# Leaving out seventeen unread products at the end of a decoder layer

## The chip, the cores and the metric

The kernel runs on one core of a Trainium2 chip. The metric is the time of one execution on the device in microseconds (us), as the median of several executions. TensorE is the matrix engine, VectorE and ScalarE work element by element, GpSimd does small element work, and SyncE's queue issues the transfers.

## The reference, cut to what matters

Eight sequences of 128 tokens with 512 features pass through one decoder layer with a layer norm behind each of three parts:

```python
x = _layernorm(x + _L0_attn_ref(x, qkvw, qkvb, ow, ob))      # 32 heads of 16 features
x = _layernorm(x + _L0_xattn_ref(x, ctx, ctx, 0, mask))      # 32 heads on 8 key and value heads
x = _layernorm(x + _L0_ffn_ref(x, weight, bias, gate_w, in_cs, out_cs))
```

The third part is a layer with ternary weights and a router over 8 experts:

```python
routing = softmax(xf @ gate_w.T)            # 8 numbers for each token
out = (xf * (routing @ in_cs)) @ sign(weight).T * (routing @ out_cs) + bias
```

## The kernel before, in words

The eight sequences go in four groups of two (i = 0 to 3). Work is split into two threads of steps. Thread A is the projections and the self attention of a group; thread B is the cross attention and the routed layer of a group. Thread C prepares weights once. `ORDER` (lines 55 to 113) is one list written by hand, in which the steps of all threads are interleaved; each engine walks through the whole list in that order and issues its own share of every step. So the order on each engine is fixed, and engines meet only at semaphores.

A step is named by thread, group, name and indices. In the last group of thread B, which is the end of the kernel, these names matter (b is the sequence in its group, u a half of the heads):

- `st`: the cross scores (line 1275), and their exponential on ScalarE (line 758)
- `pv b,u`: values by probabilities (line 1284), copied to `wide_b` by ScalarE (line 771)
- `ot b,u`: transposes of that back (`quarter`, line 1102); VectorE divides by the sums and adds the residual, and with u = 1 takes the variance (lines 994 to 1004)
- `n2 b`: the second layer norm, in halves (line 861); GpSimd takes the root (lines 605 and 609)
- `cx b,h`: transposes of x2 (line 1102), copied by ScalarE (line 794)
- `rl`, `rt`, `rr`: the router's logits (line 1297), their sum over four parts (line 1304), and the transpose of the exponentials (line 1308), with copies and an exponential on ScalarE (lines 798, 802, 805) and the maximum on VectorE (line 1011)
- `is b,h`: the routing by the input scales, contracted over 8 rows (line 1315); VectorE multiplies x2 by it (line 1024)
- `os b`: the routing by the output scales, again over 8 rows (line 1319)
- `ff b,h`: half of the output features of the ternary layer, from the high part (line 1327) and the low part (line 1331) of the input; VectorE scales, adds and takes the variance (lines 1040 to 1046)
- `n3 b`: the last layer norm and the store of the output (lines 566 and 568)

Beside the real products TensorE does unread ones. `UNREAD` (lines 116 to 129) gives for a step how many are put ahead of it, and `unread` (line 1105) issues them:

```python
held = swT if step[1] == NG - 1 and step[2] not in ("xt", "q") else wH
for _ in range(UNREAD.get(step, 0)):
    pe.matmul(dst, held[:, 0, 0:P], held[:, 0, 0:H], start=True, stop=True)
```

Each is a product of 128 x 128 by 128 x 512, written to a bank of PSUM that nobody reads before it is written again; in the profile they stand at line 1109. Behind the place `LEFT` in the list (the end of thread A) they all go to one bank that the self attention has left (lines 1122 to 1124), after a wait for that bank's last reader, which is long past in the stretch in question. The place of an unread product in TensorE's order is ahead of the real products of its step and ahead of that step's own waits.

Of the kernel before, what the change touches and what calls it, by code (L numbers as in the profile page):

```python
# [18 lines left out]
B = 8  # L19
# [26 lines left out]
def steps(table):  # L46

    out = []
    for token in table.split():
# [80 lines left out]

# [1268 lines left out]
```

## Time and profile before

| | us |
|---|---|
| median of 3 executions | 357.45 |
| lowest, highest | 356.92, 360.22 |
| the profiled execution | 357.36 |
| its span, first to last instruction | 354.9 |
| TensorE busy in the span | 330.6 |
| VectorE, ScalarE, GpSimd busy | 250.1, 191.6, 132.1 |
| mean granted clock of TensorE | 0.966 |

The profile describes one execution. Busy time of TensorE counts products whose ends are modelled and which overlap, so a busy engine is not one at its peak. The granted clock is 1.00 at the full level of 2.4 GHz and 0.50 at 1.2 GHz. The chain of work that ended last is followed back from the last instruction, at each step to what released it.

### The profile page before, as it was taken

The page shows a single profiled execution, that of the slowest core. Times are in us where ns is not written, and L with a number is a line of the kernel's source. Part 1 is how long each engine was busy: PE and PEld are TensorE (multiplying, and loading weights), DVE is VectorE, ACT ScalarE, POOL GpSimd, SP SyncE. Part 2 cuts the span into 40 slices and gives each one's busy share as a digit, 9 for nine tenths or more (in the row PEclk, how much of TensorE's full clock was granted, in tenths as well). Part 3 has the DMA queues.
Part 4 walks back from the last instruction along what each step waited for, and adds up shares of the span by engine and source line. Part 5 has one row for each costly group of instructions (what it writes and reads, how often), then busy time and mean ns, then how long its engine had stood idle before and what let it go on. Part 6 is the DMA issues. An engine that isn't in the chain of part 4 may idle for free. (4 is left out here: it accounts for less than half of the span.)

```text
span 354.9 us, 7999 instructions
## 1 busy us (share of the span) xinstructions
PE 330.6 (93%) x2835; PEld 242.5 (68%) x2835; DVE 250.1 (70%) x839; ACT 191.6 (54%) x387; POOL 132.1 (37%) x214
## 2 busy tenths in 40 slices
PE   6789989999999999999999999999989999998993
PEld 6789866688756784876576958775655676643572
DVE  2842585248998735699998347899964868898636
ACT  4923835541358758342756874316789627456420
POOL 4382462325611432343554224432226635212301
PEclk9699999999999999999999999999999999899956
DMA  7945880376951016856620165763501063200001
GB/s 269 369 162 175 246 217 5 100 208 179 235 161 36 14 35 173 229 170 144 166 86 17 28 171 163 210 155 85 134 7 37 2 166 111 85 6 0 3 0 59
DMA packets 26360, 42.77 MB, mean 121 GB/s; under 512 B 7469, under 2 KB 18361, under 8 KB 24017
## 3 DMA queue, kind: packets, MB, share of 16 engines
q1 hardware_dynamic: 26009, 41.72, 42.0%
q8 instruction: 22, 0.36, 0.4%
q10 hardware_dynamic: 312, 0.55, 0.4%
q14 instruction: 17, 0.14, 0.1%
HBM read 29.48 MB, written 12.32 MB: 118 GB/s over the span
## 5 line engine op out<-in xcount | busy, mean ns | idle before, releaser
L752 ACT ACTIVATE pa<-bank_a 128x512 f32<-128x512 f32 x64 | 35.9, 601 | 15.0 <-PE bank_a L1206 13.4
L981 DVE CUSTOM_DVE_ANT_0 x<-bank_b,mraw 128x128 bf16<-128x128 f32 x192 | 42.2, 284 | 1.0 <-PE bank_b L1264 0.8
L890 DVE TENSOR_REDUCE nma<-bank_a 128x4 f32<-128x512 f32 x64 | 40.5, 681 | 1.6 <-PE bank_a L1189 1.2
L1095 PE MATMUL bank_a<-xH,wH 128*128 128x256 f32 x128 | 36.9, 289 | 0.6 <-DVE xL L871 0.6
L1096 PE MATMUL bank_a<-xL,wH 128*128 128x256 f32 x128 | 36.0, 281 | 0.0
L1097 PE MATMUL bank_a<-xH,wL 128*128 128x256 f32 x128 | 35.9, 281 | 0.0
L758 ACT ACTIVATE pb<-bank_b 128x512 f32<-128x512 f32 x54 | 30.0, 603 | 6.6 <-PE bank_b L1275 3.7
L881 DVE SCALAR_TENSOR_TENSOR qr<-bank_a,bqk,qkp 128x256 f32<-128x256 f32 x32 | 14.0, 478 | 24.7 <-ACT qkp L723 24.7
L628 POOL TENSOR_TENSOR qkp<-qr,qkp 128x512 bf16<-128x512 f32 x16 | 18.6, 1166 | 32.1 <-DVE qkp L886 32.1
L723 ACT ACTIVATE qkp<-bank_a,bqk 128x256 bf16<-128x256 f32 x32 | 13.4, 471 | 29.9 <-PE bank_a L1097 27.1
L743 ACT ACTIVATE bank_b<-mT 128x512 f32<-128x512 f32 x48 | 27.8, 608 | 2.4 <-DVE x2T L1051 1.1
L1095 PEld LDWEIGHTS bank_a<-xH,wH 128*128 128x128 f32 x128 | 24.3, 190 | 1.0 <-DVE xL L871 0.9
L1096 PEld LDWEIGHTS bank_a<-xL,wH 128*128 128x128 f32 x128 | 24.4, 190 | 0.2
L1097 PEld LDWEIGHTS bank_a<-xH,wL 128*128 128x128 f32 x128 | 24.2, 189 | 0.0
L1220 PE MATMUL bank_a<-pa,va 128*32 128x128 f32 x512 | 23.2, 281 | 0.4 <-ACT wide_a L765 0.2
L1189 PE MATMUL bank_a<-ks,qs 96*128 96x128 bf16 x256 | 21.4, 220 | 2.0 <-DVE nma L890 1.5
L1189 PEld LDWEIGHTS bank_a<-ks,qs 96*128 96x128 bf16 x256 | 15.8, 98 | 10.5 <-issue 5.3
L605 POOL TENSOR_SCALAR rsb<-mvb 128x1 f32<-128x1 f32 x16 | 3.6, 222 | 51.9 <-DVE mvb L852 35.9
L1109 PE MATMUL bank_a<-swT 128*128 128x512 f32 x67 | 22.8, 442 | 0.0
L1206 PE MATMUL bank_a<-qs,ks 99*128 99x128 bf16 x256 | 22.1, 220 | 0.5 <-DVE x L906 0.4
L1206 PEld LDWEIGHTS bank_a<-qs,ks 99*128 99x128 bf16 x256 | 15.3, 98 | 8.9 <-issue 6.5
L1275 PE MATMUL bank_b<-qx,kx 99*128 99x512 bf16 x54 | 18.4, 384 | 1.3 <-ACT bank_b L743 0.9
(216 smaller groups left out, 825.3 us busy)
## 6 DMA issues: line engine op xcount, KB each, us to landing
scr_q<-qkp SPq DMA_DIRECT2D x8, 384.0 KB, 3.3
qs<-scr_q SPq DMA_DIRECT2D x8, 384.0 KB, 4.4
scr_k<-qkp SPq DMA_DIRECT2D x8, 384.0 KB, 2.9
ks<-scr_k SPq DMA_DIRECT2D x8, 384.0 KB, 4.7
scr_x<-xp SPq DMA_DIRECT2D x8, 384.0 KB, 2.7
qx<-scr_x SPq DMA_DIRECT2D x8, 384.0 KB, 4.0
wraw<-in_L_attn_attn_qkvw_dram SPq DMA_DIRECT2D x2, 1024.0 KB, 8.9
qs<-scr_q SPq DMA_DIRECT2D x8, 256.0 KB, 4.8
```

Source lines behind the costliest of these rows:

```text
L743: act.activation(pb_bank(i, *of)[:].rearrange("p (r t) -> p r t", r=4), held, ACT.Copy).then_inc(*rb.is_laid(i, *of))
L752: act.activation(pa[:, n % NP, :], pa_bank(i, *step)[:], ACT.Exp, scale=HD ** -0.5).then_inc(*ra.is_empty(i, *step))
L758: act.activation(pb[:, n % NPB, :], pb_bank(i, *step)[:], ACT.Exp).then_inc(*rb.is_empty(i, *step))
L890: dve.tensor_reduce(nma[:, b, 4 * j:4 * j + 4], pa_bank(i, *step)[:].rearrange("p (m t) -> p m t", m=KT), AX.X, ALU.max, negate=True).then ...
L981: last = dve.tensor_tensor_reduce(unread[:, part * P:(part + 1) * P], pb_bank(i, *step)[:, r * P:(r + 1) * P], mraw[:], -1.0, -LOWEST, ALU ...
L1095: pe.matmul(dst, lh, rh, start=kt == 0, stop=False)
L1096: pe.matmul(dst, lh, rl_, start=False, stop=False)
L1097: last = pe.matmul(dst, ll, rh, start=False, stop=kt == KT - 1)
L1109: pe.matmul(dst, held[:, 0, 0:P], held[:, 0, 0:H], start=True, stop=True)
L1189: last = pe.matmul(dst[:, m * P:(m + 1) * P], qs[0:SR, b, j, m, :], ks[0:SR, b, j, m, :], start=True, stop=True)
L1206: last = pe.matmul(dst[:, m * P:(m + 1) * P], ks[0:SM, b, j, m, :], qs[0:SM, b, j, m, :], start=True, stop=True)
L1220: last = pe.matmul(dst[m * VW:(m + 1) * VW, (j % 4) * P:(j % 4 + 1) * P], values(va, b, j * KT + m), pa[:, n % NP, m * P:(m + 1) * P], sta ...
```

## The change

In the table `UNREAD` the last nine entries are left out. They stand for seventeen unread products: two ahead of `pv` 1,1, one ahead of `ot` 1,1, two, four and two ahead of `rl`, `rt` and `rr` of sequence 0, three ahead of `cx` 1,0, one ahead of `rt` of sequence 1 and two ahead of `is` 1,0. The list of steps and everything else stay.

```diff
-          ('B', 3, 'ot', 0, 0): 4, ('B', 3, 'ot', 0, 1): 4, ('B', 3, 'st', 1, 5): 3, ('B', 3, 'pv', 1, 1): 2,
-          ('B', 3, 'ot', 1, 1): 1, ('B', 3, 'rl', 0): 2, ('B', 3, 'rt', 0): 4, ('B', 3, 'rr', 0): 2,
-          ('B', 3, 'cx', 1, 0): 3, ('B', 3, 'rt', 1): 1, ('B', 3, 'is', 1, 0): 2}
+          ('B', 3, 'ot', 0, 0): 4, ('B', 3, 'ot', 0, 1): 4, ('B', 3, 'st', 1, 5): 3}
```

## Rows read from the trace of the kernel before

**Rows 1.** The page: busy us, share, instructions of each engine; clock in 40 slices

```profile
PE 330.6 (93%) x2835; PEld 242.5 (68%) x2835; DVE 250.1 (70%) x839; ACT 191.6 (54%) x387; POOL 132.1 (37%) x214
...
PEclk9699999999999999999999999999999999899956
```

**Rows 2.** Busy time by stretch: start, end, length, engines (instructions), clock, DMA

```profile
296.80:300.00 3.20, 3.20 (x27) 2.22 (x27) 3.17 (x7) 2.27 (x5) 1.05 (x2) 1.00 0.48 139
300.20:303.40 3.20, 3.20 (x10) 2.10 (x9) 0.80 (x3) 2.59 (x6) 0.30 (x1) 0.50 0.92 260
...
330.80:334.30 3.50, 3.32 (x16) 2.11 (x16) 2.36 (x8) 1.02 (x5) 0.78 (x2) 1.00 0.00 0
334.30:337.60 3.30, 3.30 (x25) 2.08 (x24) 1.75 (x5) 2.19 (x6) 1.27 (x1) 1.00 0.01 2
337.70:341.00 3.30, 3.30 (x15) 2.58 (x14) 1.57 (x6) 0.63 (x3) 0.00 (x0) 0.50 0.00 0
```

**Rows 3.** TensorE's instructions in order of time, before the first fall

```profile
298.47 1.12 PE L1319 MATMUL bank_b<-ocf,rT 8*128 8x512 f32 x2
```

**Rows 4.** The chain that ended last, in order of time: start, us, what

```profile
332.19 0.07 DVE nl L1011
...
333.75 0.40 PE bank_a L1102 x2
...
334.47 1.08 PE bank_b L1315 x8
335.55 0.36 PE bank_b L1297 x8
335.91 1.05 PE bank_a L1319 x2
336.96 0.43 PE bank_a L1109
337.39 0.12 PE bank_b L1304 x2
337.51 0.79 PE bank_a L1327 x4
338.30 0.85 PE bank_a L1331 x4
...
340.22 1.15 PE bank_a L1315 x4
341.37 0.85 PE bank_b L1315 x4
342.22 1.71 PE bank_b L1319 x2
...
345.08 0.87 PE bank_b L1331 x4
```

**Rows 5.** Groups of instructions, 330.8 to 334.3: count, busy us, mean ns, idle

```profile
L1109 PE MATMUL bank_a<-swT 128*128 128x512 f32 x9 | 2.8, 424 | 0.0
```

**Rows 6.** TensorE's instructions in order of time, in the tail

```profile
326.34 0.71 PE L1109 MATMUL bank_a<-swT 128*128 128x512 f32 x2
327.47 1.07 PE L1284 MATMUL bank_b<-pb,vx 128*32 128x512 f32 x8 [0.42 <-ACT pb L758]
...
348.13 0.63 PE L1331 MATMUL bank_a<-swT,zL 128*128 128x256 f32 x4
```

**Rows 7.** Instructions of all engines in order of time, in the tail

```profile
328.59 0.60 ACT L771 ACTIVATE wide_b<-bank_b 128x512 f32<-128x512 f32 x1 [1.27 <-PE bank_b L1284]
...
329.34 0.63 PE L1102 MATMUL bank_a<-idf,wide_b 128*128 128x128 f32 x4
...
333.18 0.73 DVE L861 TENSOR_SCALAR x<-x,mvb,rsb 128x256 f32<-128x256 f32 x2 [0.15 <-POOL rsb L609]
...
339.40 0.27 ACT L805 ACTIVATE rT<-bank_b 8x128 f32<-8x128 f32 x1 [1.30 <-PE bank_b L1308]
```

## The prediction

> **What bounds the kernel now.** I read the page first, then the granted clock by stretches, then TensorE's own instructions in order of time over the last 30 us, and last the chain of work that ended last over the same stretch. The change touches nothing before 326 us of a span of 354.9 us, so only the last 29 us can move, apart from chance.
>
> The page's clock line shows full level nearly everywhere, with a weak spot in slice 35 and lower digits in slices 39 and 40 [rows 1]. The stretches sharpen that: the level is 0.50 from 300.2 to 303.4, is 1.00 again before the tail, stays 1.00 through 334.3 to 337.6, and is 0.50 from 337.7 [rows 2]. What TensorE did before each fall is alike: in 296.8 to 300.0 and in 334.3 to 337.6 it is marked busy throughout, but much of it is the routing products with 8 rows (lines 1315 and 1319) [rows 3, 4]. Between 330.8 and 334.3, still at full level, nine of the 16 products recorded are unread ones, 2.8 us of busy time in 3.5 us [rows 2, 5]. The reader should see there that the real work alone would be a handful of short products.
>
> The chain says which engine the end waits for. Up to about 333.7 it runs through ScalarE and VectorE (softmax copies, the second normalisation). From 333.75 to 345.95 it is TensorE almost without a break: transposes, routing products, output scales, the ternary layer's first halves [rows 4]. That is where a level of the clock is worth time.
>
> **The change part by part.** Seventeen products of 512 columns go, and with them seventeen weight loads, which lie beside products. No wait is added, no other engine's queue changes, no transfer moves.
>
> The direct gain, product by product:
> - Two before `pv` of group 1: they run at 326.34 and the real product starts at 327.47 when the exponential is ready [rows 6]. Gain 0.
> - One before `ot` 1,1: the transposes wait for ScalarE's copy that starts at 328.59 and takes 0.60, so until 329.19; they start at 329.34, so 0.15 after it [rows 7]. Gain 0, at most 0.15.
> - Two, four and two before `rl`, `rt`, `rr` of sequence 0: the logits' maximum waits its turn on VectorE behind the variance of sequence 1 and runs at 332.19 on the chain, whatever TensorE does before it [rows 4]. Gain 0.
> - Three before `cx` 1,0: they end at 333.75, and VectorE's first half of x2 ends near 333.55 (two instructions of 0.73 together from 333.18), a start latency ahead of the transposes [rows 4, 7]. Gain 0, at most 0.2.
> - One before `rt` of sequence 1: on the chain, 0.43 from 336.96. Part of that is latency that the next product would have in its place; nine unread ones take 2.8, so one is 0.31 [rows 4, 5]. Gain 0.33, between the two and nearer to the many.
> - Two before `is` 1,0: 0.85 on the chain at the lower level, but the real product then waits for ScalarE's copy of the routing weights, 339.40 + 0.27 = 339.67; with the 0.15 to start that the transposes took above, 339.82. It stands on the chain from 340.22 and its record starts at most 0.07 earlier, near 340.15 [rows 4, 7]. Gain 0.33.
>
> Sum of the direct gain: 0.66.
>
> **The price is the clock.** Without the nine products between 330.8 and 334.3 TensorE has left there the two products of `rt`, one of `rr` and the first transposes of `cx` 1,0: less than it had in either stretch before a fall [rows 2, 3, 5]. I therefore expect the level to fall between the end of the router's products (330.8) and the routing products (334.4), and to stay at 0.50 as it does from 337.7, since the work behind it is the same. How early inside that bracket matters little, as TensorE is off the chain there. The chain then pays the lower price from 334.4 to 337.7, and the same kernel shows both prices:
> - `is` of sequence 0, two steps: 1.08 at the full level; its twin for sequence 1 is 1.15 + 0.85 = 2.00 at half [rows 4]. +0.92.
> - `rl` of sequence 1: 0.36, no row at half level; between +0 and +0.36 (doubled). The routing rows come near doubling, so +0.36.
> - `os` of sequence 0: 1.05 against 1.71 [rows 4]. +0.66.
> - `rt` of sequence 1: 0.12, doubled at most. +0.12.
> - `ff` 0,0: 0.79 + 0.85 = 1.64, already mostly at half level; two such groups at 0.87 are 1.74 [rows 4]. +0.10.
> - The four transposes of `cx` 1: 0.40 for two, so 0.80 doubled adds between 0 (the fall comes behind them) and 0.80. They stand at the bracket's end; I take half, +0.40.
>
> Sum +2.56; net 2.56 - 0.66 = +1.90. Everything behind `is` 1,0 is at half level in both kernels and only shifts.
>
> The rise near the end (the last four products take 0.63 at 348.13, a group at half level 0.87 on the chain [rows 4, 6]) is unknown in both directions: if it comes later against the work, the last halves cost up to 0.35 more; if it comes earlier, `ff` 0,1 saves up to half of 1.74. I take 0, since VectorE's three instructions per half follow anyway.
>
> One row pair weighs most, for the fall's price. The rows show 1.08 against 2.00 for the same routing products at the levels 1.00 and 0.50 [rows 2, 4]. The Trainium skill, TensorE: Matmul & The Clock Gate, section "Seeing it yourself", warns that recorded clock events have been unreliable and are not to be trusted each for itself; if the fall at 337.7 were such a false record, the sum would be the direct gain alone, -0.66. The trace does not agree with that here, as the durations change with the record.
>
> Against the profiled execution (357.36 us, span 354.9, 2.5 around it) this gives 357.36 + 1.90 = **359.3**. That execution lies 0.1 from the median of 357.45, so no correction. The third run at 360.22 says that one execution can differ by 3 us without any change.
>
> **The rivals.**
> - *The level does not fall earlier.* For it: the stretch's idle time is short, and the products just before 330.8 are dense. Against it: nothing but short products is left for 3.5 us. Then only the direct gain counts, and 0.3 us more of the half-level work slips in before 337.7, worth about 0.15: 357.36 - 0.66 - 0.15 = 356.6. Chance 0.18.
> - *A little worse tail.* The fall comes before 333.7, the transposes pay all of 0.80, and the rise comes too late (+0.35): 359.3 + 0.40 + 0.35 = 360.0; with ScalarE's and VectorE's work of `ff` 0,0, which has only 0.4 us of slack before `is` 1,0, becoming late by some tenths, 360.3. Chance 0.14.
> - *Slower by over 1%: the fall comes already before `pv` 1,1 at 327.5.* The place is the pair at 326.34: without it TensorE has a gap of near 1 us there. For it: that gap. Against it: the three unread products before `st` 1,5 stay, real products follow them, and then `pv` itself. It decides if the level is 0.50 at 327.5. Price: `pv` 1.07 doubled, and eight transposes (0.40 a pair) doubled, all on the chain: 359.3 + 1.07 + 1.60 = 362.0. Chance 0.08.
> - That the edit does nothing is excluded: the loops read the table by key, and 17 records must be missing.
>
> **How the numbers follow.** Forecast 0.60, rivals 0.18, 0.14 and 0.08. About 1% (3.6 us: below 353.9, above 361.0) is what a measurement of this kernel can tell from no change. No mechanism gives 3.5 us back; 0.02 stays for faster. Slower has the third rival and the upper tail of the others: 0.11. The rest, 0.87, is within 1%. The range takes in the first rival at the low end and the second with a tail at the top: 356.4 to 361.0, leaving out the third.
>
> **What would show it.** In the changed kernel's trace: TensorE has 2818 products where it had 2835 [rows 1]; line 1109 has no row after 326.3; the granted clock is 0.50 over 334.5 to 337.5; `is` of sequence 0 takes about 2.0 instead of 1.08, and `os` 1.7 instead of 1.05; `is` 1,0 follows ScalarE's copy directly. The forecast is wrong if the clock stays 1.00 up to 337 (first rival), if it is 0.50 at 327.5 (third), or if the chain from 334 to 346 runs through ScalarE and VectorE, so that TensorE's level has no price.

## The result and the profile after

The changed kernel takes 360.08 us as the median of six executions (357.97 to 361.15), the kernel before 357.19 in the six beside it (352.93 to 360.22). The ratio is 1.010, with a 95% interval of 1.006 to 1.014: slower by about 3.6 us, forecast +1.9. The same kernel submitted once more later gave 1.0111 (1.007 to 1.0151). The median lies in the range that was given, near its top. Ratios here and below leave out executions that are over 1.5% above the fastest of the same kernel, so they are not exactly the ratio of the medians. The profiled execution of after took 360.47 us, its span is 358.4 against 354.9, 3.56 longer when the unrounded ends are taken.

The page of the kernel after, the lines that answer to [rows 1]:

```profile
PE 329.6 (92%) x2818; PEld 240.8 (67%) x2818; DVE 252.2 (70%) x839; ACT 191.9 (54%) x387; POOL 131.8 (37%) x214
...
PEclk9899999999999999999999999999999996999556
```

Seventeen products fewer, as the edit says. The tail's low digits begin in slice 38 and no longer in slice 39, and the 6 in slice 34 is another, earlier half-level stretch. The stretches of the kernel after place both (columns as in [rows 2]):

```profile
299.50:305.00 5.50, 5.50 (x20) 4.05 (x19) 2.17 (x4) 3.17 (x6) 0.51 (x1) 0.50 0.63 180
305.50:332.00 26.50, 23.92 (x156) 13.38 (x153) 23.37 (x47) 14.47 (x28) 6.72 (x15) 1.00 0.04 12
330.80:332.50 1.70, 0.75 (x11) 0.41 (x10) 1.53 (x4) 0.28 (x1) 0.61 (x1) 1.00 0.00 0
333.00:334.30 1.30, 0.37 (x1) 0.08 (x1) 0.67 (x5) 0.63 (x3) 0.78 (x2) 0.50 0.00 0
334.30:337.60 3.30, 3.04 (x16) 2.48 (x16) 0.86 (x3) 1.08 (x3) 1.26 (x1) 0.50 0.00 0
337.70:341.00 3.30, 3.30 (x14) 1.41 (x15) 1.33 (x4) 1.19 (x5) 0.00 (x0) 0.50 0.01 2
341.00:353.00 12.00, 11.04 (x43) 8.79 (x42) 6.42 (x17) 2.06 (x6) 0.79 (x2) 0.50 0.00 0
```

The level is 0.50 from before 333.0, and still at 341 to 353; before it was 1.00 through 337.6 [rows 2]. A second thing is in the first row: near 300, far ahead of the edit, the half level lasts near 7 us (298.5 to 305.3), where before it lasted 3.4. What TensorE waited for in the tail of after (waiting engine, line, what it waited for, us in total, times, longest):

```profile
PE bank_b L1306 <- ACT el L800: 1.5, 1, 1.5
PE bank_b L1282 <- ACT pb L756: 0.9, 1, 0.9
PE bank_a L1100 <- DVE x L859: 0.6, 1, 0.6
PE bank_b L1302 <- ACT lg L796: 0.5, 1, 0.5
```

These waits were mostly filled by unread products before (0.42 stayed idle ahead of `pv` [rows 6]); now TensorE idles in them, and up to `cx` the steps gain 0.06 us by it. The chain of after, in order of time (line numbers are two lower than before):

```profile
328.34 1.10 PE bank_b L1282 x8
...
334.56 0.66 PE bank_a L1100 x2
335.22 0.43 PE bank_b L1100 x2
335.64 2.00 PE bank_b L1313 x8
337.64 0.58 PE bank_b L1295 x8
338.23 2.00 PE bank_a L1317 x2
340.23 0.53 PE bank_b L1302 x2
340.76 1.05 PE bank_a L1325 x4
341.81 0.85 PE bank_a L1329 x4
...
343.32 1.19 PE bank_a L1313 x4
344.51 0.85 PE bank_b L1313 x4
345.37 1.71 PE bank_b L1317 x2
347.07 1.15 PE bank_b L1325 x4
348.22 0.85 PE bank_b L1329 x4
...
351.64 0.87 PE bank_a L1329 x4
...
352.63 0.49 DVE x2T L1038
```

Compare `is` of sequence 0: 2.00 against 1.08, and `os`: 2.00 against 1.05 [rows 4].

### The profile page after: what moved, and what is told of

The parts are those of the page before. It is cut to its first block and busy times, and to the rows that moved or that the text cites. A ratio compares the mean times of both kernels' runs of the same rounds, so it can differ in the third digit from the quotient of the medians.

```text
span 358.4 us, 7965 instructions
## 1 busy us (share of the span) xinstructions
PE 329.6 (92%) x2818; PEld 240.8 (67%) x2818; DVE 252.2 (70%) x839; ACT 191.9 (54%) x387; POOL 131.8 (37%) x214
## 5 line engine op out<-in xcount | busy, mean ns | idle before, releaser
L741 ACT ACTIVATE bank_b<-mT 128x512 f32<-128x512 f32 x48 | 27.9, 610 | 2.3 <-DVE x2T L1049 1.1
L1262 PE MATMUL bank_b<-kx,qx 96*128 96x128 bf16 x224 | 19.5, 222 | 0.2
L1273 PE MATMUL bank_b<-qx,kx 99*128 99x512 bf16 x54 | 18.4, 384 | 1.2 <-ACT bank_b L741 0.9
```

The source lines that it names most:

```text
L741: act.activation(pb_bank(i, *of)[:].rearrange("p (r t) -> p r t", r=4), held, ACT.Copy).then_inc(*rb.is_laid(i, *of))
L1262: last = pe.matmul(dst[:, r * P:(r + 1) * P], qx[0:SR, b, 4 * (g % 2) + r, g // 2, :], kx[0:SR, b, g, :], start=fresh and r == 0, stop=r = ...
```

## Where the 3.56 us of the two traces are

Each difference is the start of a step in after less its start before; the increments between them are the terms.

| step | later by | increment | forecast |
|---|---|---|---|
| `pv` 1,1 (327.47 to 328.34) to `cx` 1,0 (333.75 to 334.56) | 0.87, 0.81 | 0.81 | 0 |
| `cx` 1, four transposes | 1.17 | +0.36 | +0.40 |
| `is` of sequence 0 | 2.09 | +0.92 | +0.92 |
| `rl` of sequence 1 | 2.32 | +0.23 | +0.36 |
| `os` of sequence 0 | 3.27 | +0.95 | +0.66 |
| `rt` of sequence 1 with its unread product | 3.25 | -0.02 | +0.12 - 0.33 |
| `ff` 0,0 | 3.51 | +0.26 | +0.10 |
| up to `is` 1,0 | 3.10 | -0.41 | -0.33 |
| `is` 1, `os` 1, `ff` 0,1 | 3.13 | +0.03 | 0 |
| up to VectorE's start on the last half (349.10 to 352.63) | 3.53 | +0.40 | 0 |
| to the end of the span | 3.56 | +0.03 | 0 |

From `cx` on this is 2.75, forecast 1.90. The rest lies ahead of the first changed instruction: the exponentials ahead of `pv` 1,1 start at 326.25 before and at 327.11 after, 0.86 later, and between there and `cx` 0.05 is won back.

## The experiments

In all of them ratios are to the kernel before on the same chip, with 95% intervals, and 1% is 3.6 us. Where a time at the half level is given, it is 2 x (1 - mean granted clock) x span of each execution, averaged over all of them. "Seventeen" are the products that the change leaves out. The diffs are against the changed kernel's last line of the table, unless said otherwise.

**Which of the products matter: the eleven in the middle.**

```diff
-          ('B', 3, 'ot', 0, 0): 4, ('B', 3, 'ot', 0, 1): 4, ('B', 3, 'st', 1, 5): 3}
+          ('B', 3, 'ot', 0, 0): 4, ('B', 3, 'ot', 0, 1): 4, ('B', 3, 'st', 1, 5): 3,
+          ('B', 3, 'rl', 0): 2, ('B', 3, 'rt', 0): 4, ('B', 3, 'rr', 0): 2, ('B', 3, 'cx', 1, 0): 3}
```

> Of the seventeen, the eleven ahead of rl, rt, rr of sequence 0 and cx 1,0 are kept; the six ahead of pv 1,1, ot 1,1, rt of sequence 1 and is 1,0 are left out. Clock theory: the level stays 1.00 to about 337, the chain keeps its full-level prices (is of sequence 0 near 1.08, os near 1.05), and only the direct gain shows: 0.4 to 0.8 us below the kernel before. Rival (the whole loss lies elsewhere, for example in chance or at the earlier fall near 300): about as slow as the changed kernel, 2 to 3 us above the kernel before.

Measured: 1.0033 (0.9989 to 1.0077), 357.41 us. In its trace `is` of sequence 0 takes 1.08 and `os` 1.26, and the level falls between 338 and 339. The chain, and one of the stretches:

```profile
336.52 1.08 PE bank_b L1314 x8
...
337.96 1.26 PE bank_a L1318 x2
```

```profile
338.00:339.00 1.00, 1.00 (x2) 0.18 (x2) 0.92 (x3) 0.65 (x3) 0.00 (x0) 0.83 0.02 8
```

So the eleven give back most of the loss, which speaks against the rival. The time is a miss: the direct gain of the six left out, 0.4 to 0.8 us below the kernel before, is not there.

**The complement.**

```diff
+          ('B', 3, 'pv', 1, 1): 2, ('B', 3, 'ot', 1, 1): 1, ('B', 3, 'rt', 1): 1, ('B', 3, 'is', 1, 0): 2}
```

> The complement: the six ahead of pv 1,1, ot 1,1, rt of sequence 1 and is 1,0 are kept, the eleven between are left out. Clock theory: the level is 0.50 from before 335 on, is of sequence 0 takes 2.0 and os 1.7 to 2.0; the time is that of the changed kernel plus 0.4 to 0.9 us for the products on the chain, so 3 to 4 us above the kernel before. Rival (all products alike hold the clock, only their number counts): in between, 1 us above.

Measured: 1.0075 (1.0039 to 1.0112), 358.58 us. The tail at the half level is as forecast: the level is 0.57 on average over 334 to 335 and 0.50 from there to 344, `is` and `os` of sequence 0 take 2.00 each. One of its stretches, and its chain:

```profile
334.00:335.00 1.00, 0.79 (x4) 0.68 (x4) 0.39 (x2) 0.09 (x1) 0.00 (x0) 0.57 0.00 0
```

```profile
335.30 2.00 PE bank_b L1314 x8
...
337.88 2.00 PE bank_a L1318 x2
```

But the time, 2.7 us above the kernel before, is a miss: it is not above that of the changed kernel (1.010), rather below it, though the intervals overlap. The six seem to do more than cost. The rival's 1 us above lies below the interval, so the number of products alone does not tell the time.

**Is it the place in the queue or the work in the array?** The eleven contract over 8 rows only.

```diff
+EIGHT = (('B', 3, 'rl', 0), ('B', 3, 'rt', 0), ('B', 3, 'rr', 0), ('B', 3, 'cx', 1, 0))
+                rows = 8 if step in EIGHT else P
                 for _ in range(UNREAD.get(step, 0)):
-                    pe.matmul(dst, held[:, 0, 0:P], held[:, 0, 0:H], start=True, stop=True)
+                    pe.matmul(dst, held[0:rows, 0, 0:P], held[0:rows, 0, 0:H], start=True, stop=True)
```

All seventeen are in the table here.

> All seventeen are there as before, but the eleven ahead of rl, rt, rr and cx 1,0 contract over 8 rows and not 128, with the same 512 columns. Their time in TensorE's queue is the same. If what they give is work in the array that holds the clock, the level falls before 335 and the kernel is 2.5 to 4 us slower than before. If being issued and busy is enough, it stays 1.00 to 337 and the time is that of the kernel before within 0.5 us.

Measured: 1.0115 (1.0063 to 1.0167), 360.71 us. TensorE's instructions in order of time, from this kernel's trace:

```profile
330.30 1.21 PE L1110 MATMUL bank_a<-swT 8*128 8x512 f32 x4
...
332.76 0.97 PE L1110 MATMUL bank_a<-swT 8*128 8x512 f32 x3
```

and its stretches:

```profile
330.80:334.30 3.50, 3.42 (x16) 1.78 (x15) 1.76 (x7) 0.79 (x4) 0.78 (x2) 0.98 0.00 0
334.30:337.60 3.30, 3.30 (x18) 2.47 (x18) 1.46 (x4) 1.50 (x5) 1.26 (x1) 0.50 0.01 2
```

Four take 1.21 and three 0.97, as with 128 rows (three took 0.94), and the engine is marked busy for 3.42 of 3.50 us. The level falls all the same before 334.3, and the kernel is as slow as without the products. So filled idle time alone does not hold it. The weight loads of the eleven have 8 rows here as well, so this run does not tell the loads' part from the products'. The Trainium skill, TensorE: Matmul & The Clock Gate, section "What's actually happening", says that the half level is the default and that activity, how busy the engine has been, releases it. The runs agree on the direction; they add that the busy share as the profile marks it does not tell whether the level holds.

**Can more of them hold it longer?** The fourteen not named here stay as before, and:

```diff
+          ('B', 3, 'rl', 1): 1, ('B', 3, 'os', 0): 1, ('B', 3, 'rt', 1): 2, ('B', 3, 'rr', 1): 1,
+          ('B', 3, 'is', 1, 0): 2, ('B', 3, 'os', 1): 1, ('B', 3, 'ff', 0, 1): 1}
```

That is six more than the kernel before has, one ahead of each of these steps but `is` 1,0 (the expectation counts seven).

> The seventeen are kept and seven more are spread over the tail: one each ahead of rl and os of sequence 0 or 1 (rl 1, os 0, os 1), one more ahead of rt 1, one ahead of rr 1, one ahead of ff 0,1. Clock theory: each costs at most 0.21 to 0.33 on the chain, 1.5 to 2 us in all, and if the level stays 1.00 through 346, is and os of sequence 1 and the ff halves get 3 to 4.5 us shorter: 1 to 3 us below the kernel before. If the level falls near 338 all the same, it is 1.5 to 3 us above the kernel before.

Measured: 1.0041 (1.0007 to 1.0074), 358.12 us, a miss. Its trace shows what was hoped for:

```profile
334.30:337.60 3.30, 3.30 (x24) 1.99 (x22) 1.70 (x4) 1.76 (x5) 1.27 (x1) 1.00 0.01 2
337.70:341.00 3.30, 3.30 (x19) 2.36 (x19) 1.06 (x3) 1.23 (x4) 0.00 (x0) 1.00 0.00 0
341.00:344.50 3.50, 3.50 (x16) 2.28 (x15) 2.09 (x8) 1.34 (x3) 0.00 (x0) 0.81 0.02 5
```

and that execution is 356.36 us, the fastest of its twelve. The others reach to 362.91, with the time at the half level between 11.3 and 30.3 us. The average time at the half level is 20.5 us, against 20.4 for the kernel before: over the executions the six more do not shorten it, and their own time is what is left (1.5 us by the ratio, in which 362.61 and 362.91 do not count). One trace is one draw.

**Only the three with a price left out** (the other fourteen stay):

```diff
+          ('B', 3, 'pv', 1, 1): 2, ('B', 3, 'ot', 1, 1): 1, ('B', 3, 'rl', 0): 2, ('B', 3, 'rt', 0): 4,
+          ('B', 3, 'rr', 0): 2, ('B', 3, 'cx', 1, 0): 3}
```

> Only the three with a price on the chain are left out: one ahead of rt of sequence 1, two ahead of is 1,0; the other fourteen stay. If my direct gain is right and they do not matter for the clock: 0.4 to 0.7 us below the kernel before, the level falling near 337 to 338. If they shorten the stretch at the half level, it is as slow as the kernel before or up to 1 us slower, with the same or a longer time at the half level.

Measured: 1.0012 (0.9979 to 1.0044), 357.95 us: no gain. The average time at the half level is 23.1 us, against 20.0 for the kernel before beside it, which is what the second half of the expectation names: the three seem to matter for the clock. In the trace, TensorE's instructions in order of time:

```profile
337.40 1.19 PE L1318 MATMUL bank_a<-ocf,rT 8*128 8x512 f32 x2
338.52 0.60 PE L1303 MATMUL bank_b<-sum,lg 128*128 128x8 f32 x2
```

and the weight loads of the same kernel:

```profile
338.52 0.50 PEld L1303 LDWEIGHTS bank_b<-sum,lg 128*128 128x128 f32 x2 [0.83 <-ACT lg L797]
```

The weights of `rt` load for 0.50 at the instant at which its products start. With the unread product ahead of them this load lies beside it. Leaving it out uncovers the load. The price has to be compared at one level: at the half level the complement above, which keeps that product, has 0.72 for it and 0.23 for `rt`, where the changed kernel and this one have 0.53 for `rt` alone. So leaving it out wins 0.42 there and not 0.72. No trace has `rt` without it at the full level, at which the two took 0.43 + 0.12 [rows 4].

**Only the three ahead of `pv` and `ot` left out:**

```diff
+          ('B', 3, 'rl', 0): 2, ('B', 3, 'rt', 0): 4, ('B', 3, 'rr', 0): 2, ('B', 3, 'cx', 1, 0): 3,
+          ('B', 3, 'rt', 1): 1, ('B', 3, 'is', 1, 0): 2}
```

> Only the three ahead of pv 1,1 and ot 1,1 are left out; the other fourteen stay. Both their gain and their part in holding the clock were put at 0, so the time is that of the kernel before within 0.5 us. If they hold the clock in some executions, it is 0.5 to 1.5 us slower and the mean granted clock over the executions lower.

Measured: 0.9997 (0.9961 to 1.0033), 356.76 us, and 19.7 us at the half level on average, as in the kernel before (20.0 beside it). These three do nothing that the interval of a third of a percent would show.

**The earlier fall near 300.** All seventeen stay, and:

```diff
+          ('B', 2, 'os', 1): 2}
```

> All seventeen stay and two unread products are added ahead of os of sequence 1 of the third group, in the stretch before the earlier fall near 300. Clock theory: the two cost 0.43 us, the fall near 300 goes away in most executions and gives 1.0 to 1.7 us back: 0.5 to 1.3 us below the kernel before. Rival: the fall stays or only moves, and the kernel is 0.4 us slower.

Measured: 1.0006 (0.9972 to 1.0041), 356.38 us, a miss. The mean time at the half level goes from 20.0 to 17.6 us, so it may do something, and what it gives would be about what the two products cost. In its trace the half level near 303 is still there. No version is clearly faster than the kernel before.

**Part of the hold.** The six ahead of `rl` and `rt` of sequence 0 left out, the other eleven kept:

```diff
+          ('B', 3, 'pv', 1, 1): 2, ('B', 3, 'ot', 1, 1): 1, ('B', 3, 'rr', 0): 2, ('B', 3, 'cx', 1, 0): 3,
+          ('B', 3, 'rt', 1): 1, ('B', 3, 'is', 1, 0): 2}
```

> The six ahead of rl and rt of sequence 0 are left out, the five ahead of rr and cx 1,0 and the six others stay. Clock theory: part of the hold is gone, so in some executions the level falls before 335 and in others near 337: 0.5 to 2 us slower than before, less than the changed kernel. If the five alone hold it, it is as fast as before within 0.5 us.

Measured: 1.0034 (1.0005 to 1.0064), 357.91 us. That is 1.2 us slower, as expected of part of the hold. In its trace the level falls near 333.9, ahead of `is` of sequence 0 at 2.00, and it is up again near 344.4. How much of what it wins against the changed kernel comes from the five and how much from the six others is not separated.

**The changed kernel again, and with the last two back.** The first has no diff. The second:

```diff
+          ('B', 3, 'is', 1, 0): 2}
```

> The changed kernel once more, beside its sibling and the kernel before on one chip. In its first trace 0.87 us of the loss stood ahead of the edit, where the earlier half-level stretch lasted twice as long. If that is chance, the ratio comes out again near 1.010, the tail is 2.5 to 3.5 us longer than in the kernel before and the level falls between 331 and 335. If the tail depends on the execution, the level falls elsewhere in the second trace.

> The changed kernel with the two products ahead of is 1,0 put back, fifteen left out. By their price alone (0.40 us on the chain) it is 0.4 us slower than the changed kernel. If they bring the rise of the level forward by several us in part of the executions, it is as fast as the changed kernel or up to 1 us faster, and the mean time at the half level is 2 to 4 us shorter.

Measured: 1.0111 (1.007 to 1.0151), 360.91 us, and 1.006 (1.0017 to 1.0102), 359.51 us. In the first one's trace nothing falls near 300 (the granted clock is 1.00 from 293 to 308), the level falls between 332 and 333, and the prices are those of the first trace: `is` 2.00, `rl` 0.58, `os` 2.00, `rt` 0.53. So the longer stretch near 300 was chance and the fall in the tail was not. In this trace the tail is 2.3 us longer than in the kernel before (`cx` starts 0.08 later, the span is 2.4 longer), a little under what was expected: the level is up again between 349 and 350, and the last halves cost nothing more. The second one, although it has 0.85 of unread products at the half level on its chain, is not slower than the first: the intervals overlap, the point is 0.5% lower. Its traced execution is the fastest of its twelve (355.34 us). The stretches there:

```profile
334.30:337.60 3.30, 3.30 (x16) 1.67 (x15) 1.61 (x4) 1.00 (x3) 0.68 (x1) 0.50 0.01 2
337.70:341.00 3.30, 3.30 (x13) 2.78 (x13) 0.44 (x2) 1.12 (x4) 0.00 (x0) 0.50 0.00 0
341.00:344.50 3.50, 3.50 (x20) 2.16 (x19) 2.93 (x9) 1.52 (x4) 0.00 (x0) 0.92 0.00 0
```

and its chain:

```profile
340.59 0.21 PE bank_b L1307
340.80 0.85 PE bank_a L1108 x2
341.66 0.64 PE bank_a L1314 x4
342.29 0.45 PE bank_b L1314 x4
342.74 0.86 PE bank_b L1318 x2
343.60 0.67 PE bank_b L1326 x4
344.27 0.49 PE bank_b L1330 x4
```

Right behind the two unread products the level is up again: `is` 1 takes 1.09 instead of 2.04, `os` 0.86 instead of 1.71, `ff` 0,1 1.16 instead of 2.00. In its twelve executions the time at the half level lies between 18.4 and 33.7 us (mean 27.2); without the two, between 27.9 and 34.5 (mean 31.0, six executions).

**All runs side by side.** The average time at the half level, in us, beside that of the kernel before on the same chip:

| version | ratio | half level | kernel before |
|---|---|---|---|
| three ahead of `pv`, `ot` out | 0.9997 | 19.7 | 20.0 |
| three with a price out | 1.0012 | 23.1 | 20.0 |
| six out, eleven kept | 1.0033 | 21.6 | 20.4 |
| six ahead of `rl`, `rt` out | 1.0034 | 24.5 | 20.0 |
| eleven out, six kept | 1.0075 | 25.7 | 20.4 |
| fifteen out | 1.006 | 27.2 | 18.8 |
| eleven with 8 rows | 1.0115 | 29.0 | 20.4 |
| seventeen out, again | 1.0111 | 31.0 | 18.8 |
| two added near 300 | 1.0006 | 17.6 | 20.0 |
| six added in the tail | 1.0041 | 20.5 | 20.4 |

Among the versions that leave products out or make them smaller, those with the larger ratios are by and large those with the longer time at the half level; the two with products added pay for these beside it.

## Why the prediction was right, and where it was not

**The mechanism was right.** The level falls earlier, inside the bracket of 330.8 to 334.4 that was named (332.6 and 332.8 in the two traces of the changed kernel), and the chain pays the half-level prices from `cx` 1 to `ff` 0,0. That the eleven products in the middle do it is shown by keeping only them (1.0033, `is` of sequence 0 at 1.08) and by leaving only them out (1.0075, `is` at 2.00); the two ratios alone overlap in their intervals, the traces do not. That it is their work over 128 rows, loads included, and not their time in the queue is shown by the 8-row products (1.0115). The rival without an earlier fall (356.6) is excluded, and so is the one with a fall before 327.5: the level is 1.00 over 305.5 to 332.0. The rival with the worse tail was closest: the fall came before 333.7 in both traces, as it says, and in the first the rise came too late, for +0.40, put at 0.35 there; but the transposes cost 0.36 and not its 0.80.

**Sizes.** `is` of sequence 0 was right to the hundredth. `cx` of sequence 1 was right within 0.04 by luck: half of 0.80 was taken because the fall might come behind the transposes; it came ahead of all four, and they went from 0.40 + 0.32 to 0.66 + 0.43, by half and not to double. `os` of sequence 0 was mis-sized: 0.66 by its twin (1.71), measured 0.95. The forecast took the full price of one step (1.05, sequence 0) from the half price of another (1.71, sequence 1). Sequence 1's own full price is 0.86, in the trace with the last two back, and sequence 0's own half price is 2.00: each step nearly doubles. How the twins differ can be seen in the weight loads of the kernel before:

```profile
335.84 0.29 PEld L1319 LDWEIGHTS bank_a<-ocf,rT 8*128 8x128 f32 x2 [0.20 <-issue]
...
341.81 0.54 PEld L1319 LDWEIGHTS bank_b<-ocf,rT 8*128 8x128 f32 x2
```

For sequence 0 the load starts with its products (335.84), for sequence 1 it starts 0.21 ahead of them (342.02), beside `is`. In the trace with six more products, where one of them stands ahead of `os` of sequence 1, that step takes 1.05 at the full level as well. So what stands ahead of the step goes with its price; no run tried more of it. `rl` was 0.23, not doubled. The terms of `rt`, -0.21 net, were 0: the step doubled the products' own 0.12 and overlooked the load of 0.50 that lay beside the unread one, so that `rt` takes 0.53. `ff` 0,0 was 0.26 for 0.10: its first group takes 1.05 at the half level, not 0.87. The gain ahead of `is` 1,0 was right on the chain, 0.41 for 0.33. The rise, taken as 0, was +0.40: the last two halves run at 0.85 and 0.87 a group to the end, and now VectorE waits for TensorE at 352.63. Together 2.75 instead of 1.90. The +0.40 is not the change's own: the second trace of the changed kernel does not have it, and the trace with only the three ahead of `pv` and `ot` left out, in which the level holds past 338, ends with the same four groups of 0.85 to 0.87.

**What was missed** is the rest up to 3.6 and more, for which the many executions have to be asked. The forecast treated the clock of the profiled execution as that of the kernel. The time at the half level in the profiled one is 2 x (1 - 0.966) x 354.9 = 24 us; over 29 executions of the kernel before it is 20.4 on average, from 11.9 to 30.0, and the span follows it: the correlation is 0.89, and a line through them rises by 0.34 us of span for each us. The changed kernel has 29.8 on average (25.0 to 33.0), 9.4 more, which by that line is 3.2 us. The lowest of the changed kernel, 25.0, is above the average of the kernel before, so executions with a short time at the half level are gone; that the level comes back later in them is the likely reading, which two traces can't show. The two products ahead of `is` 1,0, booked as pure cost, may have a part in that: their return costs 0.41 on the chain at the half level and yet the kernel is not slower, and four of the traces with them (the complement, the part of the hold, the one with two products near 300, and the last one) show the level up again between 341 and 345, while in the others with them, and in all without them, it is not up before 346.5. That is a tendency and not shown: it rests on single traces, and the intervals of the ratios overlap. There is also a rival: in three of these four the level fell early, between 331 and 334.2, and stayed down for 10 to 11 us, which is about as long as in the kernels with the eleven alone and without the three with a price, where it fell past 338 without the pair. An early rise can follow from the early fall. For the pair speak the averages over executions: 27.2 with it against 31.0 without.

The stated chance of 0.11 for slower by over 1% was low: the point is 1.0% in one set of runs and 1.1% in the other. The sum should have been made for the kernel's typical execution and not for the one shown; the spread of 3.3 us in three executions was a sign of it, and was read as noise.

## What to carry to other kernels

The unread products that stood where TensorE waits cost next to nothing, and their worth was read not where they stand but several us later, from steps at both levels of the clock. A step is best compared with itself: a twin behind other products can have another price. Taking an unread product out can also uncover the weight load beside it, so both rows, products and loads, have to be read. Where the clock's level changes from execution to execution, compare the granted clock over many executions before a difference of two traces is taken for the effect.

## What was not expected of the hardware

- The scatter of this kernel, 353.20 to 360.25 us in 29 executions, goes with the clock: 0.34 us of span for each us at the half level, correlation 0.89.
- Products with 8 rows and 512 columns take as long as those with 128 rows (1.21 us for four against 1.20) and did not keep the full level.
- The same two-product step (`os`) takes 2.00 or 1.71 us at the half level and 1.05 or 0.86 at the full one, by what stands ahead of it; in the kernel before its weight load starts with its products in the dearer case and 0.21 ahead of them in the cheaper.
